# Two attention stages with their TensorE products cut into four 32-column strips

## The chip, the cores and the metric

The kernel runs on one core of a Trainium2 chip. The metric is the device time of one execution in microseconds; below stand the median of three runs and one execution taken by the hardware profiler.

## The reference

Inputs are x of 8 batches x 1024 tokens x 256 features and the weights of two attentions and of one mixture of experts. Four residual stages follow one another, each on the layer norm of what came before:

```python
x = x + attn_a(layernorm(x), ...)   # 16 heads of 16; each token looks back by 40 fixed offsets (0..32, 48, 64, ..., 384), gate, output projection
x = x + ffn(layernorm(x), ...)      # 32 experts, each takes its 8 best tokens of a batch
x = x + attn_b(layernorm(x), ...)   # 16 heads of 16, causal attention over all 1024 tokens, output projection
x = x + ffn(layernorm(x), ...)
```

Both attentions take a softmax over scores q k, the first with a bias for each offset.

## The kernel before

Each engine has a program of its own, written out step by step from one list (`band_schedule`, `dense_schedule`); semaphores order the engines against each other. Work goes by batch `b` (8) and group `g` of four heads (4), so each attention stage has 32 periods. PSUM holds three slots of 128 x 1024 fp32 and the output accumulator. Every step of TensorE that fills a slot waits until the step three before it has been taken out by VectorE or ScalarE (`slot_free`).

*Precision.* q and k are split into three bf16 parts; six pairs of parts stand on 96 partitions, so that one bf16 product gives a score in near fp32 precision. Three further partitions (99 in all) hold ones and the negated row maximum in three parts: the maximum is subtracted within the product. Projections, value products and transposes are fp32; an fp32 matmul is two records in the trace, each with a weight load and two passes over the moving columns.

*First attention* (`band_attention`). A step `mx` (maxima) puts the bias and a mask into the slot by three products with an identity (L629, L632: 128 stationary columns), then adds the scores of near tokens, 32 blocks of 32 stationary columns (`products`, L582), and those of the far offsets, 16 blocks of 64 stationary columns (L587). VectorE reduces the maxima. A step `S` does the same products transposed, without the three first. Per period: four of each, then the value products `PV` (L665, L675: fp32, 17 stationary columns a head, one head to each of the four 32-partition strips of the accumulator). `fp` (L639) sorts the far maxima, `mt` (L648) turns the maxima into rows, and DMAs (SyncE's queue) put the rows into the operands of the next group's `S`. Between the value products stand quarters of projections of the next batch or the last one (`quarter`: q and k L595, v, gate and output L603, their bias L604 by a product of 3 rows and 128 columns). GpSimd and ScalarE reorder the operands by residue (L512, L888).

*Second attention* (`dense_attention`). Units of 1024 score columns: for each group 18 units `S` (99 rows) and 18 units `mx` (96 rows) of the next group. Unit 0 has the eight diagonal tiles (L1209, 128 columns each, for `mx` after two mask products, L1205); the others have products of 128 to 512 moving columns (L1217). ScalarE takes the exponential of each `S`, VectorE the maxima of each `mx`; `PV` (L1237) is as in the first stage, 17 columns a head in four strips. Projections are L1255 (q, k), L1266 (v), L1298 (output) with biases L1268 and L1300; `mt` (L1274) is one transpose of 96 columns.

Of the kernel before, what the change touches and what calls it, by code (L numbers as in the profile page):

```python
# [18 lines left out]
P = 128  # L19
F32 = mybir.dt.float32  # L20
BF16 = mybir.dt.bfloat16
# [4 lines left out]
B, N, D = 8, 1024, 256  # L26
NT = N // P
KD = D // P
H, HD = 16, 16
G, HG = 4, 4  # L30
PARTS = 3
# [72 lines left out]
LINKS = 16  # L104
RES = N // LINKS
NEAR = [off for off in OFFSETS if off <= BLK]
FAR = [off for off in OFFSETS if off > BLK]
LINE_N, LINE_F = 96, 128


def hold(eng, sem, n):
# [118 lines left out]
def band_attention(nc, x, x_sb, stats, ident, w, scratch):  # L230
# [26 lines left out]
    with ExitStack() as ctx:  # L257
# [3 lines left out]
        wqk = sb("wqk", [P, 2, KD, H, HD])  # L261
        wv = sb("wv", [P, KD, D])
        wout = sb("wout", [P, KD, D])
# [4 lines left out]
        bias_rows = row_home[0:PARTS, 0, 0:3 * D].rearrange("a (n d) -> a n d", n=3)  # L268
        ones_rows = row_home[0:PARTS, 1, 0:P]
        neg_rows = row_home[AT_ROWS:AT_ROWS + HG * PARTS, :, :]  # L270
        ident16 = sb("ident16", [P, P], BF16)
        bias_k = sb("bias_k", [P, H, 2, 64])
        bias_q = [sb(f"bias_q{kind}", [P, H, 64], BF16) for kind in range(2)]
        before_first = sb("before_first", [P, 64], BF16)
        perm = sb("perm", [P, P + LINKS], BF16)
# [198 lines left out]
        with nc.Block() as block:  # L474
# [85 lines left out]
            def _(pe):  # L560
# [14 lines left out]
                def products(dst, rows, h, left, right, ahead, start):  # L575

                    for blk in range(N // BLK):
                        i, c = divmod(blk, 4)
                        lo = BLK * blk - (0 if ahead else BLK)
                        first, last = max(lo, 0), min(lo + 64, N)  # L580
                        at = 64 * i - lo
                        pe.matmul(dst[BLK * c:BLK * (c + 1), at + first:at + last], left[0][rows, h, BLK * blk:BLK * (blk + 1)],  # L582
                                  right[0][rows, h, first:last], start=start, stop=True, skip_group_check=True)
                    for r in range(LINKS):
                        pair, r2 = divmod(r, 2)
                        at = 512 + 64 * pair
                        ins = pe.matmul(dst[RES * r2:RES * (r2 + 1), at:at + 64], left[1][rows, h, RES * r:RES * (r + 1)],  # L587
                                        right[1][rows, h, RES * r:RES * (r + 1)], start=start, stop=True, skip_group_check=True)
                    return ins

                def quarter(dst, kind, b, part, n):

                    if kind in ("q", "k"):
                        kd, c = divmod(n, 2)
                        return pe.matmul(dst[:, c * 512:(c + 1) * 512],  # L595
                                         wqk[:, "qk".index(kind), kd, 8 * part:8 * part + 8, :].rearrange("p h d -> p (h d)"),
                                         zT[:, kd, c * 512:(c + 1) * 512], start=kd == 0, stop=kd == KD - 1)
                    weights, bias = {"v": (wv, V_BIAS), "gate": (wgate, GATE_BIAS), "op": (wout, OUT_BIAS)}[kind]
                    to = dst[:, n * D:(n + 1) * D]
                    for kd in range(KD):  # L600
                        tokens = flatT[:, (n * KD + kd) * P:(n * KD + kd + 1) * P] if kind == "op" else \
                            zT[:, kd, (4 * part + n) * P:(4 * part + n + 1) * P]
                        pe.matmul(to, tokens, weights[:, kd, :], start=kd == 0, stop=False)  # L603
                    return pe.matmul(to, ones_rows[:, :], bias_rows[:, bias, :], start=False, stop=True)  # L604

                def stacks(b, g, pair):
                    near, far = ring(b, g, pair, BY_TOKEN), ring(b, g, pair, BY_RESIDUE)
# [2 lines left out]
                for step in seq:  # L610
# [8 lines left out]
                    elif kind == "mx":  # L619
# [6 lines left out]
                        pe.wait_ge(turned_k, turns)  # L626
                        dst = slot_free(step)
                        for kind in range(2):
                            pe.matmul(dst[:, 512 * kind:512 * (kind + 1)], ident16[:, :],  # L629
                                      bias_q[kind][:, HG * g + h, :].unsqueeze(1).to_broadcast([P, NT, 64]), start=True, stop=False,  # L630
                                      skip_group_check=True)
                        pe.matmul(dst[:, 0:64], ident16[:, :], before_first[:, :], start=False, stop=False, skip_group_check=True)  # L632
                        products(dst, slice(0, QK_ROWS), h % 2, q, k, False, False).then_inc(filled, 1)
                    elif kind == "fp":
                        _, b, g = step
                        pe.wait_ge(spread_steps, 3 * count("fparts", "fparts", b, g))
                        dst = slot_free(step)
                        for pair in range(NT):
                            ins = pe.matmul(dst[:, 0:64], perm[:, LINKS - 2 - 2 * pair:LINKS - 2 - 2 * pair + P], far_parts[:, pair, :, :].rearrange("p t c -> p (t c)"),  # L639
                                            start=pair == 0, stop=pair == NT - 1)  # L640
                        ins.then_inc(filled, 1)
                    elif kind == "mt":
                        _, b, g = step
# [389 lines left out]
def dense_attention(nc, x_sb, stats, ident, w, scratch):  # L1033
# [32 lines left out]
    with ExitStack() as ctx:  # L1066
# [53 lines left out]
        with nc.Block() as block:  # L1120
# [56 lines left out]
            def _(pe):  # L1177
# [11 lines left out]
                for step in seq:  # L1189
# [3 lines left out]
                    if kind in ("S", "mx"):  # L1193
# [8 lines left out]
                        own, other, rows = (k_stack[n], q_stack[n], ALL_ROWS) if kind == "S" else (q_stack[n], k_stack[n], QK_ROWS)  # L1202
                        if u == 0:
                            for c in range(2 if kind == "mx" else 0):
                                pe.matmul(dst[:, 512 * c:512 * (c + 1)], ident16[:, :], later[:, :].unsqueeze(1).to_broadcast([P, 4, P]),  # L1205
                                          start=True, stop=False, skip_group_check=True)
                            for tile in range(NT):
                                mine = slice(P * tile, P * tile + P)
                                ins = pe.matmul(dst[:, mine], own[0:rows, h, mine], other[0:rows, h, mine], start=kind == "S", stop=True,  # L1209
                                                skip_group_check=True)  # L1210
                        for head, base in ((h, 0),) if 0 < u < 4 else ((2 * h, 0), (2 * h + 1, 512)) if u else ():
                            for tile, at in (unit_tiles if kind == "S" else unit_maxima)(u):
                                at += base
                                lo, end = (P * tile + P, N) if kind == "S" else (0, P * tile)
                                while lo < end:
                                    top = min(end, lo + 512 - at % 512)
                                    ins = pe.matmul(dst[:, at:at + top - lo], own[0:rows, head, P * tile:P * tile + P],  # L1217
                                                    other[0:rows, head, lo:top], start=True, stop=True)
                                    at, lo = at + top - lo, top
                        ins.then_inc(filled, 1)  # L1220
                    elif kind == "PV":
# [27 lines left out]
                    elif kind in ("q", "k"):  # L1249
# [2 lines left out]
                        dst = slot_free(step)  # L1252
                        for kd in range(KD):
                            for c in range(2):
                                ins = pe.matmul(dst[:, c * 512:(c + 1) * 512],  # L1255
                                                wqk[:, "qk".index(kind), kd, 8 * half:8 * half + 8, :].rearrange("p h d -> p (h d)"),
                                                zT[:, kd, c * 512:(c + 1) * 512], start=kd == 0, stop=kd == KD - 1)
                        ins.then_inc(filled, 1)
                    elif kind == "v":
                        _, b, i4 = step  # L1260
# [2 lines left out]
                        for i in range(4):  # L1263
                            tile = slice((4 * i4 + i) * P, (4 * i4 + i + 1) * P)
                            for kd in range(KD):
                                pe.matmul(dst[:, i * D:(i + 1) * D], zT[:, kd, tile], wv[:, kd, :, :].rearrange("p h d -> p (h d)"),  # L1266
                                          start=kd == 0, stop=False)
                            ins = pe.matmul(dst[:, i * D:(i + 1) * D], ones_rows[:, :], bias_rows[:, V_BIAS, :], start=False, stop=True)  # L1268
                        ins.then_inc(filled, 1)
                    elif kind == "mt":  # L1270
                        _, b, g = step
                        pe.wait_ge(mred_done, count("mred", "mred", b, g))
                        dst = slot_free(step)
                        pe.transpose(dst[:, :].bitcast(BF16)[0:PARTS * HG * NT, 0:P], neg_parts[:, :, :, :].rearrange("p a h i -> p (a h i)"),  # L1274
                                     ident16[:, :]).then_inc(filled, 1)
                    elif kind == "ot":
                        _, b, g = step
                        pe.wait_ge(ote_done, count("ote", "ote", b, g))
# [13 lines left out]
                    elif kind == "op":  # L1292
                        _, b, i4 = step
                        pe.wait_ge(taken_act, count("taken_act", "at", b, i4))
                        dst = slot_free(step)
                        for i in range(4):
                            for kd in range(KD):
                                pe.matmul(dst[:, i * D:(i + 1) * D], flatT[:, (i * KD + kd) * P:(i * KD + kd + 1) * P], wout[:, kd, :],  # L1298
                                          start=kd == 0, stop=False)
                            ins = pe.matmul(dst[:, i * D:(i + 1) * D], ones_rows[:, :], bias_rows[:, OUT_BIAS, :], start=False, stop=True)  # L1300
                        ins.then_inc(filled, 1)

            @block.vector
# [748 lines left out]
```

## Time and profile before

| | us |
|---|---|
| median of 3 runs (lowest, highest) | 3425.82 (3421.61, 3429.7) |
| span of the profiled execution | 3413.9 |
| TensorE matmul busy | 2844.6 (83%), 45724 matmuls |
| VectorE, ScalarE, GpSimd busy | 1633.9 (48%), 1439.6 (42%), 811.5 (24%) |
| first attention, main part | 120 to 1337 |
| second attention, main part | 1760 to 3115 |

In the trace's rows a time of a matmul reaches from its start to its modelled end, so that matmuls overlap; how fast they follow each other is read from the starts. A form like `99*128 99x512 bf16` is rows * stationary columns, then rows x moving columns.

### The profile page before, as it was taken

The page shows a single profiled execution, that of the slowest core. Times are in us where ns is not written, and L with a number is a line of the kernel's source. Part 1 is how long each engine was busy: PE and PEld are TensorE (multiplying, and loading weights), DVE is VectorE, ACT ScalarE, POOL GpSimd, SP SyncE. Part 2 cuts the span into 40 slices and gives each one's busy share as a digit, 9 for nine tenths or more (in the row PEclk, how much of TensorE's full clock was granted, in tenths as well). Part 3 has the DMA queues.
Part 4 walks back from the last instruction along what each step waited for, and adds up shares of the span by engine and source line. Part 5 has one row for each costly group of instructions (what it writes and reads, how often), then busy time and mean ns, then how long its engine had stood idle before and what let it go on. Part 6 is the DMA issues. An engine that isn't in the chain of part 4 may idle for free. (4 is left out here: it accounts for less than half of the span.)

```text
span 3413.9 us, 101201 instructions
## 1 busy us (share of the span) xinstructions
PE 2844.6 (83%) x45724; PEld 1618.9 (47%) x45724; DVE 1633.9 (48%) x2745; ACT 1439.6 (42%) x1425; POOL 811.5 (24%) x567
## 2 busy tenths in 40 slices
PE   2678888978888886799569899998989899997897
PEld 1455565656556565434334444444444444443444
DVE  2444343344344443600666666666666666663401
ACT  1454444444534443410235454555545554554401
POOL 3343433343434331000412122222222221210002
PEclk9789898889889897899679999999999999998998
DMA  6332323243333331388042122222222221221397
GB/s 182 87 101 66 95 66 97 70 107 77 94 79 80 82 93 36 115 326 365 19 92 58 44 57 55 57 57 57 57 57 57 56 58 40 56 39 58 152 420 268
DMA packets 233548, 344.23 MB, mean 101 GB/s; under 512 B 113691, under 2 KB 142181, under 8 KB 216741
## 3 DMA queue, kind: packets, MB, share of 16 engines
q1 hardware_dynamic: 207892, 310.02, 31.2%
q10 hardware_dynamic: 25232, 27.83, 3.4%
q8 instruction: 357, 5.85, 0.7%
q14 instruction: 67, 0.54, 0.1%
HBM read 266.15 MB, written 69.24 MB: 98 GB/s over the span
## 5 line engine op out<-in xcount | busy, mean ns | idle before, releaser
L1362 DVE TENSOR_REDUCE b_tops<-b_slot 128x8 f32<-128x1024 f32 x576 | 680.1, 1219 | 358.1 <-PE b_slot L1217 180.6
L1403 ACT ACTIVATE b_probs<-b_slot 128x1024 f32<-128x1024 f32 x576 | 583.0, 1023 | 550.7 <-PE b_slot L1217 396.3
L512 POOL COPY a_q_far<-a_q_near 96x1024 bf16<-96x1024 bf16 x128 | 259.1, 2054 | 344.4 <-PE a_slot L587 218.6
L1164 POOL TENSOR_SCALAR_AFFINE_SELECT b_probs<-b_probs 128x1024 f32<-128x1024 f32 x128 | 139.8, 1093 | 808.1 <-ACT b_probs L1403 808.1
L1237 PE MATMUL b_outT_ps<-b_probs,b_v 128*17 128x128 f32 (+3 forms) x4608 | 319.4, 385 | 6.2 <-ACT b_probs L1403 5.6
L1217 PE MATMUL b_slot<-b_q_stack,b_k_stack 99*128 99x512 bf16 (+3 forms) x1280 | 275.6, 322 | 43.5 <-DVE b_tops L1362 32.8
L888 ACT ACTIVATE a_k_far<-a_k_near 96x1024 bf16<-96x1024 bf16 x128 | 258.3, 2068 | 102.7 <-DMA a_k_near<-parts_near_dram 93.6
L1217 PE MATMUL b_slot<-b_k_stack,b_q_stack 96*128 96x512 bf16 (+3 forms) x1280 | 266.7, 323 | 29.4 <-DVE b_tops L1362 20.6
L788 DVE TENSOR_TENSOR a_probs<-a_slot,a_bias_k 128x1024 f32<-128x1024 f32 x128 | 154.4, 1217 | 182.9 <-PE a_slot L587 182.7
L797 DVE TENSOR_REDUCE a_tops<-a_slot 128x16 f32<-128x1024 f32 x128 | 156.3, 1221 | 135.9 <-PE a_slot L587 134.9
L851 ACT ACTIVATE a_probs<-a_probs 128x1024 f32<-128x1024 f32 x128 | 133.3, 1053 | 176.3 <-DVE a_probs L788 153.8
L1217 PEld LDWEIGHTS b_slot<-b_q_stack,b_k_stack 99*128 99x128 bf16 x1280 | 107.1, 100 | 204.7 <-DVE b_tops L1362 61.8
L1896 PE MATMUL f_ps<-f_w_ring,f_hidT 128*32 128x256 f32 x1024 | 184.0, 380 | 2.1 <-ACT f_hidT L1944 2.1
L1217 PEld LDWEIGHTS b_slot<-b_k_stack,b_q_stack 96*128 96x128 bf16 x1280 | 97.5, 98 | 185.4 <-DVE b_tops L1362 61.5
L665 PEld LDWEIGHTS a_outT_ps<-a_probs,a_v_near 128*17 128x17 f32 x8448 | 129.8, 103 | 84.6 <-issue 73.9
L665 PE MATMUL a_outT_ps<-a_probs,a_v_near 128*17 128x64 f32 (+1 forms) x8448 | 153.8, 228 | 16.1 <-issue 10.9
L629 PE MATMUL a_slot<-a_bias_q,a_ident 128*128 128x512 bf16 x256 | 100.3, 482 | 80.1 <-POOL a_q_far L512 50.0
L595 PE MATMUL a_slot<-a_zT,a_wqk 128*128 128x512 f32 x256 | 149.8, 691 | 5.7 <-issue 3.0
L1875 PE MATMUL f_ps<-f_w_ring,f_lhs 128*32 128x512 f32 x512 | 146.9, 606 | 7.9 <-POOL f_lhs L1854 7.9
L1976 DVE TENSOR_TENSOR f_pre<-f_ps,f_b1T 128x128 f32<-128x128 f32 x32 | 7.8, 286 | 299.9 <-PE f_ps L1884 299.9
L1237 PEld LDWEIGHTS b_outT_ps<-b_probs,b_v 128*17 128x17 f32 x4608 | 96.3, 96 | 113.8 <-issue 69.3
L675 PE MATMUL a_outT_ps<-a_probs,a_v_far 128*17 128x32 f32 x8192 | 110.5, 198 | 37.1 <-issue 36.7
(226 smaller groups left out, 4262.0 us busy)
## 6 DMA issues: line engine op xcount, KB each, us to landing
f_w_ring<-in_L_ffn_w_dram SPq DMA_DIRECT2D x128, 1024.0 KB, 9.9
parts_near_dram<-a_parts ACTq DMA_DIRECT2D x96, 256.0 KB
parts_dram<-b_parts SPq DMA_DIRECT2D x96, 256.0 KB
a_k_near<-parts_near_dram SPq DMA_DIRECT2D x128, 128.0 KB, 3.0
b_k_stack<-parts_dram SPq DMA_DIRECT2D x64, 256.0 KB, 6.8
a_q_near<-parts_near_dram SPq DMA_DIRECT2D x64, 192.0 KB, 2.9
b_q_stack<-parts_dram SPq DMA_DIRECT2D x32, 384.0 KB, 4.5
values_dram<-a_v_stage SPq DMA_DIRECT2D x16, 544.0 KB, 3.8
```

Of the source, the lines that this page charges most:

```text
L512: pool.tensor_copy(q_far[far][0:QK_ROWS, h, :].rearrange("p (r a) -> p r a", r=LINKS), q_near[near][0:QK_ROWS, h, :].rearrange("p (a r) -> ...
L595: return pe.matmul(dst[:, c * 512:(c + 1) * 512], wqk[:, "qk".index(kind), kd, 8 * part:8 * part + 8, :].rearrange("p h d -> p (h d)"), zT ...
L665: ins = pe.matmul(outT_ps[BLK * h:BLK * h + HD + 1, lo:top], v_near[:, c, blk % 4, (HD + 1) * h:(HD + 1) * (h + 1)], probs[h][:, at:at + t ...
L788: ins = dve.tensor_tensor(probs[h][:, :].rearrange("p (k t c) -> p k t c", k=2, c=64), src[:, :].rearrange("p (k t c) -> p k t c", k=2, c=64),
L797: ins = dve.tensor_reduce(tops[:, h, :, :].rearrange("p k t -> p (k t)"), src[:, :].rearrange("p (t c) -> p t c", c=64), AX.X, ALU.max)
L888: act.activation(k_far[far][0:QK_ROWS, h, :].rearrange("p (r a) -> p r a", r=LINKS), k_near[near][0:QK_ROWS, h, :].rearrange("p (a r) -> p ...
L1217: ins = pe.matmul(dst[:, at:at + top - lo], own[0:rows, head, P * tile:P * tile + P], other[0:rows, head, lo:top], start=True, stop=True)
L1237: ins = pe.matmul(outT_ps[32 * h:32 * h + HD + 1, first:last], v1[b % 2][:, j, HG * g + h, :], src[:, base + first:base + last], start=u = ...
L1362: ins = dve.tensor_reduce(out, src, AX.X, ALU.max)
L1403: act.activation(probs_of(b, g, u, h)[:, :], slot_of(step)[:, :], ACT.Exp).then_inc(taken_act, 1)
L1875: ins = pe.matmul(bank[n][32 * j:32 * j + 32, :], lhs1[half][:, kd, j, :], w1_ring[:, j, kd, n * 512:(n + 1) * 512], start=kd == 0, stop=k ...
L1896: ins = pe.matmul(bank[4 + half][32 * j:32 * j + 32, 0:D], hidT[half][:, c, j, :], w2_ring[:, j, c, :], start=c == 0, stop=c == HE // P - 1)
```

## The change

A helper issues one product as four: 32 stationary columns each, to the four strips of 32 partitions of the same PSUM tile, with the same moving operand. It replaces the products of L595, L603, L629, L632, L639, L1205, L1209, L1217, L1255, L1266 and L1298; the far products (L587) go from one of 64 columns to two of 32, and the second stage's `mt` from one transpose to three. The bias products, all other transposes, the value products and the expert stages stay.

```diff
+STRIP = 32
+def strips(pe, dst, left, right, start, stop, skip=False):
+    for c in range(0, P, STRIP):
+        ins = pe.matmul(dst[c:c + STRIP], left[:, c:c + STRIP], right, start=start, stop=stop, skip_group_check=skip)
+    return ins
...
-                        ins = pe.matmul(dst[RES * r2:RES * (r2 + 1), at:at + 64], left[1][rows, h, RES * r:RES * (r + 1)],
-                                        right[1][rows, h, RES * r:RES * (r + 1)], start=start, stop=True, skip_group_check=True)
+                        for half in range(0, RES, STRIP):
+                            to = RES * r2 + half
+                            ins = pe.matmul(dst[to:to + STRIP, at:at + 64], left[1][rows, h, RES * r + half:RES * r + half + STRIP],
+                                            right[1][rows, h, RES * r:RES * (r + 1)], start=start, stop=True, skip_group_check=True)
...
-                        pe.matmul(to, tokens, weights[:, kd, :], start=kd == 0, stop=False)
-                    return pe.matmul(to, ones_rows[:, :], bias_rows[:, bias, :], start=False, stop=True)
+                        strips(pe, to, tokens, weights[:, kd, :], kd == 0, False, True)
+                    return pe.matmul(to, ones_rows[:, :], bias_rows[:, bias, :], start=False, stop=True, skip_group_check=True)
...
-                                ins = pe.matmul(dst[:, mine], own[0:rows, h, mine], other[0:rows, h, mine], start=kind == "S", stop=True,
-                                                skip_group_check=True)
+                                ins = strips(pe, dst[:, mine], own[0:rows, h, mine], other[0:rows, h, mine], kind == "S", True, True)
...
-                                    ins = pe.matmul(dst[:, at:at + top - lo], own[0:rows, head, P * tile:P * tile + P],
-                                                    other[0:rows, head, lo:top], start=True, stop=True)
+                                    ins = strips(pe, dst[:, at:at + top - lo], own[0:rows, head, P * tile:P * tile + P],
+                                                 other[0:rows, head, lo:top], True, True, True)
...
-                        pe.transpose(dst[:, :].bitcast(BF16)[0:PARTS * HG * NT, 0:P], neg_parts[:, :, :, :].rearrange("p a h i -> p (a h i)"),
-                                     ident16[:, :]).then_inc(filled, 1)
+                        for a in range(PARTS):
+                            ins = pe.transpose(dst[:, :].bitcast(BF16)[STRIP * a:STRIP * a + HG * NT, 0:P],
+                                               neg_parts[:, a, :, :].rearrange("p h i -> p (h i)"), ident16[:, :])
+                        ins.then_inc(filled, 1)
...
```

The other products named above are replaced by `strips` in the same way.

## Rows read from the trace of the kernel before

**Rows 1.** Busy time by stretch: span of it, engines' busy us (instructions), clock, DMA share, GB/s.

```profile
120.00:1337.00 1217.00, 1009.07 (x30732) 694.95 (x30736) 523.80 (x785) 551.50 (x427) 434.74 (x273) 0.88 0.33 83
...
1760.00:3115.00 1355.00, 1232.66 (x10585) 604.56 (x10576) 844.76 (x1171) 698.22 (x701) 254.83 (x180) 0.99 0.24 52
```

**Rows 2.** Waits of TensorE, 1760 to 3115: who for whom, us in all, times, longest.

```profile
PE b_slot L1217 <- DVE b_tops L1362: 49.8, 118, 0.5
```

**Rows 3.** Waits of TensorE, 120 to 1337.

```profile
PE a_slot L582 <- DMA a_q_far<-a_row_home: 43.9, 16, 10.1
PE a_slot L629 <- POOL a_q_far L512: 35.4, 15, 5.4
PE a_outT_ps L675 <- issue: 32.0, 33, 2.3
...
PE a_outT_ps L665 <- issue: 10.9, 11, 1.9
```

**Rows 4.** Timeline of TensorE in the second attention: start, us, form, count, idle before.

```profile
2208.34 0.61 PE L1217 MATMUL b_slot<-b_q_stack,b_k_stack 99*128 99x512 bf16 x3 [0.35 <-DVE b_tops L1362]
2208.88 0.84 PE L1237 MATMUL b_outT_ps<-b_probs,b_v 128*17 128x384 f32 x8
2209.65 0.61 PE L1217 MATMUL b_slot<-b_k_stack,b_q_stack 96*128 96x512 bf16 x3
2210.09 1.03 PE L1266 MATMUL b_slot<-b_wv,b_zT 128*128 128x256 f32 x4
2211.06 0.28 PE L1268 MATMUL b_slot<-b_bias_rows,b_ones_rows 3*128 3x256 bf16 x1
2211.26 1.13 PE L1266 MATMUL b_slot<-b_wv,b_zT 128*128 128x256 f32 x4
2212.33 0.28 PE L1268 MATMUL b_slot<-b_bias_rows,b_ones_rows 3*128 3x256 bf16 x1
```

**Rows 5.** Timeline of TensorE in the first attention, two places.

```profile
841.38 0.41 PE L582 MATMUL a_slot<-a_q_near,a_k_near 99*32 99x64 bf16 x32
841.73 0.44 PE L587 MATMUL a_slot<-a_q_far,a_k_far 99*64 99x64 bf16 x16
842.10 0.61 PE L629 MATMUL a_slot<-a_bias_q,a_ident 128*128 128x512 bf16 x2
...
897.91 1.12 PE L595 MATMUL a_slot<-a_zT,a_wqk 128*128 128x512 f32 x2
898.97 1.99 PE L665 MATMUL a_outT_ps<-a_probs,a_v_near 128*17 128x64 f32 x136
```

**Rows 6.** Instruction queue q8, 120 to 1337, then 1760 to 3115: packets, MB, share.

```profile
q8 instruction: 242, 3.96, 1.4%
...
q8 instruction: 84, 1.38, 0.4%
```

**Rows 7.** Timeline of TensorE at the end of the first attention.

```profile
1326.78 0.36 PE L665 MATMUL a_outT_ps<-a_probs,a_v_near 128*17 128x64 f32 x16 [1.60 <-issue]
1327.08 0.41 PE L639 MATMUL a_slot<-a_far_parts,a_perm 128*128 128x64 bf16 x8
1327.42 1.12 PE L675 MATMUL a_outT_ps<-a_probs,a_v_far 128*17 128x32 f32 x104
1330.35 0.37 PE L675 MATMUL a_outT_ps<-a_probs,a_v_far 128*17 128x32 f32 x24 [1.82 <-issue]
...
1333.92 0.54 PE L675 MATMUL a_outT_ps<-a_probs,a_v_far 128*17 128x32 f32 x41 [1.75 <-issue]
```

**Rows 8.** Timeline of TensorE, two stalls, 128 matmuls from the first to the second.

```profile
906.45 0.59 PE L595 MATMUL a_slot<-a_zT,a_wqk 128*128 128x512 f32 x1 [1.35 <-issue]
...
910.31 0.89 PE L675 MATMUL a_outT_ps<-a_probs,a_v_far 128*17 128x32 f32 x74 [0.36 <-issue]
```

**Rows 9.** Busy time by group of one batch (g = 0 to 3), columns as in rows 1.

```profile
757.60:801.00 43.40, 40.75 (x1044) 29.05 (x1044) 17.59 (x20) 18.20 (x15) 14.00 (x9) 0.96 0.36 89
801.00:841.40 40.40, 36.10 (x1005) 23.90 (x1005) 16.80 (x26) 19.91 (x16) 14.08 (x9) 0.87 0.26 58
841.40:883.50 42.10, 31.58 (x979) 20.66 (x979) 17.74 (x27) 18.98 (x15) 18.23 (x11) 0.80 0.41 105
883.50:913.80 30.30, 22.99 (x960) 16.55 (x964) 14.52 (x18) 15.30 (x12) 11.47 (x8) 0.94 0.38 95
```

More of the change, by code:

```diff
@@ L594, in quarter @@
                         kd, c = divmod(n, 2)
-                        return pe.matmul(dst[:, c * 512:(c + 1) * 512],
-                                         wqk[:, "qk".index(kind), kd, 8 * part:8 * part + 8, :].rearrange("p h d -> p (h d)"),
-                                         zT[:, kd, c * 512:(c + 1) * 512], start=kd == 0, stop=kd == KD - 1)
+                        return strips(pe, dst[:, c * 512:(c + 1) * 512],
+                                      wqk[:, "qk".index(kind), kd, 8 * part:8 * part + 8, :].rearrange("p h d -> p (h d)"),
+                                      zT[:, kd, c * 512:(c + 1) * 512], kd == 0, kd == KD - 1, True)
                     weights, bias = {"v": (wv, V_BIAS), "gate": (wgate, GATE_BIAS), "op": (wout, OUT_BIAS)}[kind]
@@ L628, in _ @@
                         for kind in range(2):
-                            pe.matmul(dst[:, 512 * kind:512 * (kind + 1)], ident16[:, :],
-                                      bias_q[kind][:, HG * g + h, :].unsqueeze(1).to_broadcast([P, NT, 64]), start=True, stop=False,
-                                      skip_group_check=True)
-                        pe.matmul(dst[:, 0:64], ident16[:, :], before_first[:, :], start=False, stop=False, skip_group_check=True)
+                            strips(pe, dst[:, 512 * kind:512 * (kind + 1)], ident16[:, :],
+                                   bias_q[kind][:, HG * g + h, :].unsqueeze(1).to_broadcast([P, NT, 64]), True, False, True)
+                        strips(pe, dst[:, 0:64], ident16[:, :], before_first[:, :], False, False, True)
                         products(dst, slice(0, QK_ROWS), h % 2, q, k, False, False).then_inc(filled, 1)
@@ L638, in _ @@
                         for pair in range(NT):
-                            ins = pe.matmul(dst[:, 0:64], perm[:, LINKS - 2 - 2 * pair:LINKS - 2 - 2 * pair + P], far_parts[:, pair, :, :].rearrange("p t c -> p (t c)"),
-                                            start=pair == 0, stop=pair == NT - 1)
+                            ins = strips(pe, dst[:, 0:64], perm[:, LINKS - 2 - 2 * pair:LINKS - 2 - 2 * pair + P],
+                                         far_parts[:, pair, :, :].rearrange("p t c -> p (t c)"), pair == 0, pair == NT - 1, True)
                         ins.then_inc(filled, 1)
@@ L1204, in _ @@
                             for c in range(2 if kind == "mx" else 0):
-                                pe.matmul(dst[:, 512 * c:512 * (c + 1)], ident16[:, :], later[:, :].unsqueeze(1).to_broadcast([P, 4, P]),
-                                          start=True, stop=False, skip_group_check=True)
+                                strips(pe, dst[:, 512 * c:512 * (c + 1)], ident16[:, :], later[:, :].unsqueeze(1).to_broadcast([P, 4, P]),
+                                       True, False, True)
                             for tile in range(NT):
                                 mine = slice(P * tile, P * tile + P)
-                                ins = pe.matmul(dst[:, mine], own[0:rows, h, mine], other[0:rows, h, mine], start=kind == "S", stop=True,
-                                                skip_group_check=True)
+                                ins = strips(pe, dst[:, mine], own[0:rows, h, mine], other[0:rows, h, mine], kind == "S", True, True)
                         for head, base in ((h, 0),) if 0 < u < 4 else ((2 * h, 0), (2 * h + 1, 512)) if u else ():
@@ L1254, in _ @@
                             for c in range(2):
-                                ins = pe.matmul(dst[:, c * 512:(c + 1) * 512],
-                                                wqk[:, "qk".index(kind), kd, 8 * half:8 * half + 8, :].rearrange("p h d -> p (h d)"),
-                                                zT[:, kd, c * 512:(c + 1) * 512], start=kd == 0, stop=kd == KD - 1)
+                                ins = strips(pe, dst[:, c * 512:(c + 1) * 512],
+                                             wqk[:, "qk".index(kind), kd, 8 * half:8 * half + 8, :].rearrange("p h d -> p (h d)"),
+                                             zT[:, kd, c * 512:(c + 1) * 512], kd == 0, kd == KD - 1, True)
                         ins.then_inc(filled, 1)
@@ L1265, in _ @@
                             for kd in range(KD):
-                                pe.matmul(dst[:, i * D:(i + 1) * D], zT[:, kd, tile], wv[:, kd, :, :].rearrange("p h d -> p (h d)"),
-                                          start=kd == 0, stop=False)
-                            ins = pe.matmul(dst[:, i * D:(i + 1) * D], ones_rows[:, :], bias_rows[:, V_BIAS, :], start=False, stop=True)
+                                strips(pe, dst[:, i * D:(i + 1) * D], zT[:, kd, tile], wv[:, kd, :, :].rearrange("p h d -> p (h d)"),
+                                       kd == 0, False, True)
+                            ins = pe.matmul(dst[:, i * D:(i + 1) * D], ones_rows[:, :], bias_rows[:, V_BIAS, :], start=False, stop=True,
+                                            skip_group_check=True)
                         ins.then_inc(filled, 1)
@@ L1297, in _ @@
                             for kd in range(KD):
-                                pe.matmul(dst[:, i * D:(i + 1) * D], flatT[:, (i * KD + kd) * P:(i * KD + kd + 1) * P], wout[:, kd, :],
-                                          start=kd == 0, stop=False)
-                            ins = pe.matmul(dst[:, i * D:(i + 1) * D], ones_rows[:, :], bias_rows[:, OUT_BIAS, :], start=False, stop=True)
+                                strips(pe, dst[:, i * D:(i + 1) * D], flatT[:, (i * KD + kd) * P:(i * KD + kd + 1) * P], wout[:, kd, :],
+                                       kd == 0, False, True)
+                            ins = pe.matmul(dst[:, i * D:(i + 1) * D], ones_rows[:, :], bias_rows[:, OUT_BIAS, :], start=False, stop=True,
+                                            skip_group_check=True)
                         ins.then_inc(filled, 1)
```

## The prediction

> **What bounds the kernel now.** I read the busy time by stage first, then who TensorE waits for in the two attention stages, then the timeline of a few microseconds of each, and last the DMA queues. The two attention stages take 1217 and 1355 of the 3414 us, and TensorE is busy 83% and 91% of them; no other engine passes 62% [rows 1]. In the second stage what TensorE does wait for is small pieces: 118 waits on one reduction of VectorE, 50 us in all, 0.5 us the longest [rows 2]. So there TensorE sets the pace, and time taken from it is mostly time won. The first stage differs: beside waits for the transposed maxima (DMA, 44 us) there are waits put down to "issue", where the engine had nothing to wait for and still did not go on: 32 and 11 us at the two lines of the value products alone [rows 3].
>
> The reader should now find in the timeline what a change of array shape costs. A step of 1024 score columns takes 0.44 us to the next start when a full-width product follows (2209.65 to 2210.09), which is its streaming, 1024 columns at 2.4 GHz = 0.43; it takes 0.54 when a 17-column product follows (2208.34 to 2208.88). Back again, eight records of 384 fp32 columns need 0.64 in two rounds (384 x 2 / 2.4 GHz each) and take 0.77 [rows 4]. So a change of shape costs 0.10 us. The eight records also show that four strips run side by side: one after another they would need 2.56 us.
>
> **What goes.** Along the timeline I count the places where neighbouring matmuls differ in shape (at most 32, 64 or 128 stationary columns; 3 rows or about 100): 1403 in the first stage, 987 in the second. With the change 513 and 406 are left: transposes stay at 128 columns, and the bias product keeps 3 rows and 128 columns, with a change on either side. Removed are 890 and 581, at 0.098 us: 87 and 57 us.
>
> The first fp32 weight load after a shape change isn't hidden: four records start to finish 0.97 us behind a full-width step and 1.07 behind the bias product [rows 4]; a woven quarter of a projection takes 1.06 for 0.85 of streaming, 0.10 of it the change of shape back [rows 5]. A 32-column load behind a change costs at most the 0.03 left over in the 0.77 above. I count 238 and 90 such loads: at 0.075 us 18 and 7 us (ends: 0 and 0.10 each).
>
> Streaming stays: four strips pass the same moving columns side by side, as the value products do in fp32 and the near products in bf16 (32 matmuls of 64 columns in 0.35 us to the next start, against 0.85 one after another; the 16 of 64 stationary columns in 0.37) [rows 5]. Three transposes for one in the second stage's row step, 32 times, I put at nothing: they go to three strips. So TensorE is relieved of 105 us in the first stage and of 64 in the second.
>
> **What is added: instructions.** Every strip is a weight load and a matmul of its own. One instruction queue moves in step with TensorE, whatever the others do: 242 packets of 16.4 KB for the 30732 matmuls of the first stage, one for 127 matmuls, 84 for the 10585 of the second [rows 6, 1]. What a packet costs when it is late is seen at the end of the first stage: three stalls put down to "issue", at 1326.78, 1330.35 and 1333.92, and between the first two exactly 16 + 8 + 104 = 128 matmuls: 3.57 us a packet, of which the engine worked about half [rows 7]. A second pair, at 906.45 and 910.31, again 128 matmuls apart, gives 3.86 [rows 8]. I take the mean, 3.72; these are the ends of the price.
>
> Matmuls added in one group of four heads in the first stage: 8 steps x 16 far products, 4 maxima steps x 9, 24 in the far maxima: 188; and 24 for each q or k, 48 for each v, gate or output half. The four groups of a batch have 8, 4, 3 and 1 units of 24 of these: 192, 96, 72, 24. From 1044, 1005, 979 and 960 [rows 9] that makes 1424, 1289, 1239 and 1172 matmuls, or 11.1, 10.1, 9.7 and 9.2 packets. At 3.72 us: 41.4, 37.5, 36.0 and 34.1 us, against periods of 43.4, 40.4, 42.1 and 30.3 now [rows 9]. The fourth is the tell-tale: it has the least other work, and its 7.5 packets x 3.72 = 27.9 us already fill 92% of its 30.3. If a stream bound by its packets keeps that 8.6% of pauses (waits in which nothing is drawn), the four become 45.0, 40.7, 39.1 and 37.0: 161.8 us for the batch's 156.2. The 13.1 us that a batch is relieved of (111 shape changes, 30 loads) don't come off again: where packets set the pace, they are already spent inside these numbers, and the third group without packets, 42.1 less its share of 3.8, would end at 38.3, under its 39.1. First stage: +5.6 x 8 = +45 us.
>
> What the Trainium skill says of this (Runtime: NRT & Kernel Launch, section Instruction fetch mechanics): the sequencer fetches the next block of 256 instructions by its own DMA while the current one runs, and crossing into it is mostly hidden. The block's size agrees with 127 matmuls a packet; the stalls of 1.6 to 1.8 us do not agree with hidden. By the rule this term would be 0, the first stage would win, and the sum is that of the first rival.
>
> Second stage: each group has 40 + 32 matmuls of scores, the same of maxima and 8 of mask, all four-fold, and its projections; some 530 more in 42 us, so 84 packets become about 216 in 1355 us, 6.3 us apiece, far from 3.9. The relief counts here. Not in full: VectorE is busy 62% of the stage, and TensorE stands behind its reductions in 118 of its 1152 steps already (18 of each kind in 32 groups) [rows 1, 2]; each step that comes sooner meets them more often. I take two thirds of 64, -43 us (ends: a third and all, -21 and -64). The expert stages don't change.
>
> Sum against the profiled span of 3413.9: +45 - 43 = +2, so 3416; the median of the runs lies 11.9 us above that span, hence **3428 us**.
>
> **Rivals.** *Packets stay hidden.* The extra packets land where TensorE waits for something else. Then the first stage gives two thirds of its 105, -70, and the whole is 3426 - 70 - 43 = 3313. Even with packets at the low price and no pause, three of four groups come out under their present length. For: 44 us of DMA waits and 35 of GpSimd's in rows like these can cover packets [rows 3]. Against: the fourth group, 92% full.
>
> *Packets cost more.* At 3.86 us with the same pauses a batch takes 167.9 us, +11.7 x 8 = +94; if VectorE also keeps two thirds of the second stage's relief, 3426 + 94 - 21 = 3499. It decides as soon as a packet costs over 3.72 us, the price at which both stages cancel. For: the stage runs at a DMA share of 0.33 [rows 1], the cheap pair stood in a quiet stretch.
>
> *Strips load one after another.* If the four 32-column loads of a 128-column product don't overlap, 128 moving columns (0.053 us at 2.4 GHz) cost the 0.10 of an exposed load: for the 2560 such products of the second stage +0.047 each = +120 us, 3548. Against: 32 loads and matmuls in 0.35 us [rows 5]. The Trainium skill (TensorEngine Tiling (Array Packing), Feature Incompatibilities) does say that column tiling excludes the fast weight load; no row here shows a cost of it.
>
> *The shape change is paid anyway*, since numbers of rows (96, 99, 128) or types also count as a shape: the rows deny it (fp32 behind bf16 at full width took 0.44) [rows 4].
>
> **How the numbers follow.** Cancelling within 40 us either way: 0.46 (own range 3388 to 3468). Hidden packets: 0.22. Dear packets: 0.26. Loads in turn: 0.04. No shape change removed: 0.02, no change. What a measurement of this kernel can tell from no change is about 0.2%, 7 us. Of the first case 0.18 falls below that, 0.10 inside, 0.18 above. Faster 0.40, same 0.12, slower 0.48. The range from 3350 to 3490 leaves the far part of the two big rivals out.
>
> **What would show it.** In the profile after: second stage, score step to value product 0.43 instead of 0.54, the stage some 40 us shorter, VectorE's share up. First stage: over 300 packets, "issue" waits of TensorE well above now, 128 matmuls between stalls, the fourth group 36 to 38 us, the third 38 to 40. Wrong if the "issue" waits don't grow, if strips show 0.2 us or more for four of 512 columns one after another, or if the second stage doesn't shorten because VectorE's reductions end last.

## The result, and the profile after

The changed kernel takes 3584.03 us (median of 4 runs, 3574.83 to 3605.45) against 3423.72: ratio 1.0479, 95% interval 1.044 to 1.0519. Forecast were 3428 us, 3350 to 3490. The profiled execution's span is 3576.6 us, 162.7 more than before.

The page, TensorE's busy time and the instruction queue:

```profile
PE 2779.1 (78%) x71772; PEld 1617.0 (45%) x71772; DVE 1637.9 (46%) x2745; ACT 1436.1 (40%) x1425; POOL 813.2 (23%) x567
...
q8 instruction: 560, 9.18, 1.1%
```

TensorE is busy 65 us less than before, and the kernel is 163 us longer: time was lost while the array stood still. By stretch, the two attentions, then one batch's four groups of the first, the same batch as in [rows 9]:

```profile
120.00:1415.00 1295.00, 954.80 (x39261) 655.69 (x39262) 527.08 (x785) 551.90 (x426) 435.71 (x273) 0.86 0.31 79
1845.00:3285.00 1440.00, 1223.81 (x26788) 653.71 (x26781) 846.01 (x1172) 694.92 (x702) 255.95 (x181) 0.95 0.23 50
...
789.93:840.31 50.38, 40.77 (x1425) 25.40 (x1426) 17.60 (x20) 18.30 (x15) 13.81 (x9) 0.90 0.32 81
840.31:882.37 42.06, 32.40 (x1286) 21.47 (x1289) 16.62 (x26) 19.94 (x16) 14.13 (x9) 0.92 0.22 53
882.37:923.96 41.59, 27.51 (x1240) 19.50 (x1232) 17.85 (x27) 18.12 (x14) 18.32 (x11) 0.88 0.41 107
923.96:959.13 35.17, 23.07 (x1168) 17.19 (x1168) 14.24 (x18) 16.32 (x13) 11.47 (x8) 0.85 0.33 83
```

Against [rows 1] the first attention is 78 us longer and the second 85; what lies outside the two takes 842 us in both. In the first TensorE's busy time fell by 54 us and its idle time (length less busy) rose from 208 to 340; in the second it went from 122 to 216. The waits name it, of the first attention (120 to 1415), then of the second (1845 to 3285):

```profile
PE a_slot L597 <- issue: 72.1, 36, 3.7
PE a_outT_ps L684 <- issue: 65.4, 47, 2.7
PE a_slot L590 <- issue: 51.0, 32, 4.2
PE a_outT_ps L674 <- issue: 29.0, 36, 1.9
...
PE a_slot L115 <- issue: 20.8, 21, 2.5
...
PE b_slot L115 <- issue: 70.8, 25, 5.2
PE b_slot L115 <- DVE b_tops L1374: 53.5, 130, 0.6
...
PE b_outT_ps L1245 <- issue: 14.7, 5, 4.3
```

(L590 and L597 are the near and far products, L674 and L684 the value products, L115 is the helper; L1245 is L1237 of before.) "Issue" had 32 and 11 us at the value products of the first attention [rows 3], 60 in all its rows there, and no row in the second. Now it has 238 us in the five rows of the first (249 in all) and 86 in the second, where VectorE's row hardly moved [rows 2]. The packets of q8 in the same two stretches, against 242 and 84 [rows 6]:

```profile
q8 instruction: 308, 5.05, 1.7%
...
q8 instruction: 210, 3.44, 1.0%
```

What the strips do to the array is as forecast. A score step is followed by a value product after 0.44 us, where it was 0.54 [rows 4], and the four strips of 512 columns pass side by side:

```profile
2270.49 0.61 PE L115 MATMUL b_slot<-b_q_stack,b_k_stack 99*32 99x512 bf16 x12
2270.93 1.04 PE L1245 MATMUL b_outT_ps<-b_probs,b_v 128*17 128x128 f32 x32
```

The end of the first attention, as in [rows 7]: the stalls follow each other at 3.74, 3.62, 3.60 and 3.47 us, a packet's 127 or 128 matmuls apart, so the price of a late packet held too:

```profile
1396.60 1.88 PE L674 MATMUL a_outT_ps<-a_probs,a_v_near 128*17 128x64 f32 x128 [0.24 <-issue]
1400.34 1.36 PE L674 MATMUL a_outT_ps<-a_probs,a_v_near 128*17 128x64 f32 x87 [1.87 <-issue]
...
1403.96 1.25 PE L684 MATMUL a_outT_ps<-a_probs,a_v_far 128*17 128x32 f32 x120 [1.88 <-issue]
...
1407.56 0.46 PE L657 MATMUL a_slot<-a_ident,a_neg_parts 128*12 128x128 bf16 x6 [1.93 <-issue]
...
1411.03 0.26 PE L684 MATMUL a_outT_ps<-a_probs,a_v_far 128*17 128x32 f32 x9 [1.80 <-issue]
```

**One long stall of the second attention.** At the beginning of each group the eight steps of unit 0 follow each other: 32 strips of 128 columns for each `S`, 8 + 32 for each `mx`. Timelines of TensorE and of SyncE's DMA issues, then the DMA queues from 2249.6 to 2254.7 and from 2254.7 to 2257.0, then busy time in three stretches (the last three columns are granted clock, DMA share and GB/s):

```profile
2247.72 0.63 PE L115 MATMUL b_slot<-b_q_stack,b_k_stack 99*32 99x128 bf16 x32 [0.43 <-DMA b_q_stack<-b_neg_rows]
...
2252.13 0.61 PE L115 MATMUL b_slot<-b_q_stack,b_k_stack 99*32 99x128 bf16 x30
2257.91 0.29 PE L115 MATMUL b_slot<-b_q_stack,b_k_stack 99*32 99x128 bf16 x2 [5.16 <-issue]
2257.91 1.14 PE L115 MATMUL b_slot<-b_later,b_ident 128*32 128x512 bf16 x8
2258.74 2.02 PE L115 MATMUL b_slot<-b_k_stack,b_q_stack 96*32 96x128 bf16 x44
2260.45 1.16 PE L115 MATMUL b_slot<-b_q_stack,b_k_stack 99*32 99x128 bf16 x32
2261.30 1.16 PE L115 MATMUL b_slot<-b_k_stack,b_q_stack 96*32 96x512 bf16 x12
```

```profile
2244.61 0.76 SPq L1161 DMA_DIRECT2D b_q_stack<-b_neg_rows  x1
2245.88 1.27 SPq L1156 DMA_DIRECT2D b_q_stack<-parts_dram  x3
2247.19 1.84 SPq L1156 DMA_DIRECT2D b_k_stack<-parts_dram  x4
```

```profile
q1 hardware_dynamic: 552, 0.98, 107.0%
...
q8 instruction: 1, 0.02, 4.5%
```

```profile
2249.60:2254.70 5.10, 3.14 (x146) 2.10 (x136) 3.26 (x3) 1.94 (x2) 2.08 (x2) 1.00 1.07 193
2254.70:2257.90 3.20, 0.00 (x0) 0.00 (x0) 0.00 (x0) 0.00 (x0) 0.00 (x0) 0.76 0.27 37
2257.90:2263.20 5.30, 5.29 (x114) 3.72 (x117) 3.06 (x3) 2.05 (x2) 1.56 (x2) 0.50 0.01 3
```

Read it in this order. The burst begins as the rows of maxima arrive, at 2247.72, and from 1.8 us ahead of it until 1.3 us into it SyncE issues seven stack loads of the group after next. TensorE passes a packet boundary at some 2249.6 (128 matmuls ahead of the stall). For the next 5.1 us the sixteen DMA engines move loads at 193 GB/s and queue q8 moves nothing; its packet starts only as they run out, at 2254.75 by the trace's records, and 3.2 us later TensorE goes on. The clock, 1.00 ahead of the stall, is 0.50 behind it (1.2 for 2.4 GHz): the 44 strips at 2258.74 take 2.02 us from first start to last end, and the same 44 take 1.24 in e5 below, without a stall. In the changed kernel 22 stalls of the second attention are over 2 us, 77 us of the 86. In each the packet started 2.8 to 6.7 us behind the last boundary, with 140 to 210 GB/s of transfers between. They fall at the group's first steps (18) or some 10 us later (4): in every second group SyncE issues stores of the next batch's q and k (L1144) right behind the rows of maxima, and the stack loads 9 to 10 us behind them instead of 1.3; three of the 18 fall behind such stores.

### The profile page after: what moved, and what is told of

Same layout as the page of the kernel before. It is cut to its first block and busy times, and to the rows that moved or that the text cites. A ratio compares the mean times of both kernels' runs of the same rounds, so it can differ in the third digit from the quotient of the medians.

```text
span 3576.6 us, 153297 instructions
## 1 busy us (share of the span) xinstructions
PE 2779.1 (78%) x71772; PEld 1617.0 (45%) x71772; DVE 1637.9 (46%) x2745; ACT 1436.1 (40%) x1425; POOL 813.2 (23%) x567
## 5 line engine op out<-in xcount | busy, mean ns | idle before, releaser
L115 PE MATMUL b_slot<-b_q_stack,b_k_stack 99*32 99x128 bf16 (+3 forms) x9216 | 378.5, 284 | 73.2 <-issue 27.2
L115 PE MATMUL b_slot<-b_k_stack,b_q_stack 96*32 96x128 bf16 (+3 forms) x9216 | 375.3, 287 | 65.1 <-issue 37.8
L1245 PE MATMUL b_outT_ps<-b_probs,b_v 128*17 128x128 f32 (+3 forms) x4608 | 323.0, 386 | 25.1 <-issue 14.7
L115 PEld LDWEIGHTS b_slot<-b_k_stack,b_q_stack 96*32 96x32 bf16 x9216 | 208.0, 101 | 223.5 <-issue 91.5
L115 PEld LDWEIGHTS b_slot<-b_q_stack,b_k_stack 99*32 99x32 bf16 x9216 | 194.3, 100 | 248.4 <-issue 82.9
L674 PE MATMUL a_outT_ps<-a_probs,a_v_near 128*17 128x64 f32 (+1 forms) x8448 | 172.9, 234 | 31.8 <-issue 29.0
L674 PEld LDWEIGHTS a_outT_ps<-a_probs,a_v_near 128*17 128x17 f32 x8448 | 153.7, 107 | 86.3 <-issue 79.2
L684 PE MATMUL a_outT_ps<-a_probs,a_v_far 128*17 128x32 f32 x8192 | 116.7, 200 | 70.5 <-issue 70.1
L1245 PEld LDWEIGHTS b_outT_ps<-b_probs,b_v 128*17 128x17 f32 x4608 | 120.5, 99 | 84.4 <-ACT b_probs L1415 36.7
L115 PE MATMUL a_slot<-a_bias_q,a_ident 128*32 128x512 bf16 x1024 | 109.2, 506 | 60.7 <-POOL a_q_far L520 43.4
L115 PE MATMUL a_slot<-a_zT,a_wqk 128*32 128x512 f32 x1024 | 146.0, 641 | 3.8 <-issue 2.4
```

The source lines that it names most:

```text
L115: ins = pe.matmul(dst[c:c + STRIP], left[:, c:c + STRIP], right, start=start, stop=stop, skip_group_check=skip)
L674: ins = pe.matmul(outT_ps[BLK * h:BLK * h + HD + 1, lo:top], v_near[:, c, blk % 4, (HD + 1) * h:(HD + 1) * (h + 1)], probs[h][:, at:at + t ...
L1245: ins = pe.matmul(outT_ps[32 * h:32 * h + HD + 1, first:last], v1[b % 2][:, j, HG * g + h, :], src[:, base + first:base + last], start=u = ...
```

## The experiments

All are ratios to the kernel before in runs on the same chip (3423 to 3427 us there), with 95% intervals.

| run | us | ratio |
|---|---|---|
| e1 first attention changed alone | 3492.02 | 1.0223 (1.0184 to 1.0263) |
| e2 second attention changed alone | 3505.19 | 1.0253 (1.0203 to 1.0302) |
| e3 = e2, stack loads later in the order | 3506.03 | 1.0243 (1.0201 to 1.0285) |
| e4 = e2, unit 0 at 128 columns | 3404.86 | 0.9943 (0.9922 to 0.9965) |
| e5 = e2, stack loads held | 3403.45 | 0.9931 (0.9909 to 0.9953) |
| e6 kernel before, stack loads held | 3430.16 | 1.0019 (1.0 to 1.0037) |
| e7 = e1, far products at 64 columns | 3446.58 | 1.0059 (1.0037 to 1.008) |
| e8 = e4, stack loads held | 3385.84 | 0.9883 (0.9856 to 0.9909) |
| e9 whole change, stack loads held | 3479.28 | 1.0167 (1.0139 to 1.0195) |
| e10 only projection quarters of the first | 3416.80 | 0.9979 (0.9961 to 0.9997) |
| e11 = e8 + e10 | 3375.38 | 0.9864 (0.984 to 0.9889) |
| e12 = e1, V loaded once | 3493.06 | 1.0208 (1.0184 to 1.0233) |
| e13 kernel before, V loaded once | 3420.02 | 0.9979 (0.9965 to 0.9992) |

**e1 and e2: each attention alone.** The edit: the diff in one of the two functions only.

> The change in the first attention alone. Both theories: the loss of 78 us that the two profiles show up to the end of the first attention stays and the second stage is that of before, so about 3503 us (3490 to 3515). If the two stages' losses are not independent (the first leaving a queue or a clock behind for the second), it lies elsewhere.

> The change in the second attention alone: 3424 + 84 = about 3508 us (3495 to 3520), with some 86 us of TensorE waits put down to issue in that stage and a granted clock of 0.93 to 0.95 there.

Both lose: 2.2% and 2.5%, together 4.8%, which is the whole. So the stages' losses add up, and the forecast's gain of 43 us in the second does not exist in it even by itself.

**e3: stack loads seven beats later in the written order.**

```diff
-            if ahead[0] < B:
-                seq.append(("stack",) + ahead)
...
+                if n == 6 and ahead[0] < B:
+                    seq.append(("stack",) + ahead)
```

> The change in the second attention alone, and the loads of a group's operand stacks (1.3 MB for the group after the next) issued at the seventh of its 18 beats instead of ahead of the first, where the instructions come densest. Theory of late instruction packets, held up by these loads on the same DMA engines: the issue waits of the stage fall to less than half, the half-clock stretches behind them too, 3440 to 3470 us. Rival, the strips themselves cost TensorE time (moving operand read four times, weight loads that do not overlap): as the second attention alone, 3500 to 3515 us.

Nothing moved, which looks like the end of the theory. But the experiment was empty. SyncE's queue isn't paced by the beats, only by its semaphores, and the loads were issued where they had been, behind the rows of maxima (at this burst of the changed kernel 1.27 us, here the same; in the other groups within 0.2 us of e2):

```profile
2178.93 0.76 SPq L1161 DMA_DIRECT2D b_q_stack<-b_neg_rows  x1
2180.20 1.27 SPq L1156 DMA_DIRECT2D b_q_stack<-parts_dram  x3
```

**e4: unit 0 and its mask back to 128 columns.** The edit: the `strips` of `u == 0` become the products of before; 6912 of the 16960 added matmuls go.

> The change in the second attention alone, but with unit 0 (mask products and the eight diagonal tiles of each head) left at 128 columns: of 16900 added matmuls 6900 stay away, those of the densest beats, and most shape changes beside the value products are still gone. Late packets: next to no issue waits, the relief of some 40 us shows, 3385 to 3400 us. Strips that cost TensorE time: 10000 added matmuls remain, no gain, 3440 us or more.

From 82 us slower to 18 faster, 5 us above the range expected, while the strips of all other units stay. The loss comes with the strips of unit 0, whose score products are the shortest; 14 us of stalls are left (10.1 at the helper, 4.3 at the value products).

**e5 and e6: the loads really kept out of the burst**, in e2 and, as a control, in the kernel before. The edit is the order of e3 and this wait:

```diff
+                        if now := before(b, g, 2):
+                            sp.wait_ge(filled, count("filled", "S", *now, 1, 2))
```

> Second attention changed alone, and the loads of the stacks two groups ahead really kept out of the burst: SyncE waits, ahead of each stack load, for the products of the group's seventh beat. In the kernel with the late place in the order these loads had still started at the group's first beat (2180.2 us, 1.3 us behind the rows of maxima), since nothing paced SyncE; that run moved nothing and told nothing. Theory A, the loads hold the instruction packet back (in the stalls of over 2 us the packet started 2.4 to 5.8 us behind the last boundary, with 178 to 212 GB/s of loads between): the long stalls at the group's first beats go, 3425 to 3455 us. Theory B, a packet has its price whatever the loads do: 3500 to 3510 us, as without the hold.

> The kernel before with the same hold on the stack loads and nothing else, as a control. Theory A and B alike: 84 packets in the second attention were all there in time, so the hold is worth nothing, 3415 to 3430 us. If the hold itself costs (stacks late for the next group's maxima), it is above 3430.

One wait on SyncE, with no instruction taken from TensorE, brings e2 from 3505 to 3403 us, further than I expected; in the kernel before the same wait is worth nothing (3430.16, at the upper end of what was expected). The same burst in e5, with the loads issued 20 us behind the rows of maxima, then the waits for the helper (1760 to 3115) and the second attention as a whole:

```profile
2143.60 0.63 PE L115 MATMUL b_slot<-b_q_stack,b_k_stack 99*32 99x128 bf16 x32 [0.43 <-DMA b_q_stack<-b_neg_rows]
...
2148.01 0.62 PE L115 MATMUL b_slot<-b_q_stack,b_k_stack 99*32 99x128 bf16 x32
2148.45 0.61 PE L115 MATMUL b_slot<-b_later,b_ident 128*32 128x512 bf16 x8
2148.89 1.24 PE L115 MATMUL b_slot<-b_k_stack,b_q_stack 96*32 96x128 bf16 x44
```

```profile
2140.50 0.76 SPq L1163 DMA_DIRECT2D b_q_stack<-b_neg_rows  x1
2160.53 1.26 SPq L1158 DMA_DIRECT2D b_q_stack<-parts_dram  x3
```

```profile
PE b_slot L115 <- issue: 16.2, 15, 2.3
```

```profile
1680.40:3127.00 1446.60, 1259.44 (x27871) 661.70 (x27871) 895.35 (x1224) 714.40 (x721) 276.50 (x192) 0.97 0.26 55
```

In e2 the waits on issue are 74.9 + 11.1 us and the same stretch, first slot to last, is this:

```profile
1678.50:3218.80 1540.30, 1288.94 (x27871) 682.55 (x27871) 895.95 (x1224) 713.57 (x721) 276.44 (x192) 0.94 0.24 52
```

So 94 us shorter: about 70 of stalls, and the clock can account for the rest. Summed over the trace's clock records, this stretch has 171 us at half clock in e2 and 95 in e5 (89 in the kernel before, 198 in the changed one). At half clock a step of 32 strips took 0.85 us to the next start (2260.45 to 2261.30 above), at full clock 0.44, so the 76 us are worth some 38 at most. Three stalls of 2.1 to 2.3 us are left in e5, in groups where the stores of q and k run during the burst; the wait doesn't hold those.

**e7: far products of the first attention at 64 columns**, `products` as before the change.

> First attention changed alone, but with the products of the far keys left at 64 columns: 4096 fewer matmuls than the 9100 or so added, 32 packets fewer, and up to 512 shape changes come back. Theory, packets set the pace of the first attention at some 3.7 us each: 32 packets are worth 60 to 118 us and the shapes cost 26 to 51 us, so 3400 to 3460 us against 3492. Rival, the strips themselves cost array time and the packets are mostly hidden: 3515 to 3545 us.

49 of e1's 69 us go (each against its own runs of before) with 4096 matmuls, 32 packets, although up to 512 changes of shape come back: 1.5 us net a packet. TensorE's waits on issue in this stage (120 to 1415) go from 244 us in e1 to 148. The rival is out, and the array doesn't lose by the far strips either: in the changed kernel 32 of them take 0.33 us to the next start, where the 16 of 64 columns took 0.37 ahead of the same product [rows 5].

```profile
795.21 0.51 PE L597 MATMUL a_slot<-a_q_far,a_k_far 99*32 99x64 bf16 x32
795.54 0.61 PE L115 MATMUL a_slot<-a_bias_q,a_ident 128*32 128x512 bf16 x8
```

**e8 and e9: the hold beside other versions.** e8 is e4 with the hold, e9 the whole change with it.

> Second attention with unit 0 and its mask left at 128 columns, plus the hold on the stack loads. Theory A: the 14 us of stalls left there shrink a little, 3390 to 3405 us. Theory B: no change from 3405 us, 3398 to 3412.

> The whole change with the stack loads of the second attention held to the seventh beat. Theory, the hold is worth in it what it was worth in the second attention alone (3505 to 3403 us, 102 us) and the first attention keeps its own price (69 us alone): 3584 less 102 is 3482, range 3470 to 3498 us, second attention near 1450 us long, first near 1390. Rival, the two stages share one loss: above 3510.

e8 is another 19 us under e4 and under the range of either theory: e4's last 14 us of stalls in this stage are gone (no such row among the 40 largest waits). Its second attention is 1422.50 us against the 1466.2 of before from first slot to last: 44 us shorter, about what was forecast for this stage, though unit 0 keeps its shapes here; it also has 27 us less at half clock (62 for 89), worth up to half of that. e9 comes out 3 us from the sum of the parts.

```profile
1678.90:3101.40 1422.50, 1250.49 (x20959) 642.64 (x20959) 895.04 (x1224) 716.60 (x721) 276.44 (x192) 0.98 0.25 56
```

**e10 and e11: a version that beats both.** The edit of e10: `quarter` alone takes `strips`, 3072 matmuls more; e11 puts it on e8.

> The kernel before with only the woven projection quarters of the first attention in strips: 3072 matmuls more, 24 packets, and two shape changes fewer at each of up to 448 quarters. Theory, packets at 3.7 us where the pieces fall in starved stretches, hidden where a quarter's long matmuls cover them: 27 to 89 us lost, 45 to 90 us gained, so 3385 to 3440 us, likeliest 3415. Rival, strips give the array nothing: 3450 or more.

> The fastest so far (second attention with unit 0 at 128 columns and the hold, 3386 us) plus the projection quarters of the first attention in strips. 3386 plus whatever the quarters alone change against the kernel before: 3345 to 3400 us, likeliest 3375.

e10 gains a little (0.2%, the interval ends at 0.9997). e11 is the fastest kernel of the study: 1.4% under the kernel before, 5.8% under the changed one.

**e12 and e13: the first attention without most loads of V.** SyncE loads V for the first group only and every later group multiplies by that V, so the output is another.

```diff
+                        if (b, g) != (0, 0):
+                            continue
...
-                            pe.wait_ge(v_in, VIN * count("vin", "vin", b, g))
+                            pe.wait_ge(v_in, VIN)
```

> First attention changed alone, with the loads of V into the near and far layouts made for the first group only; later groups reuse the first group's V, so the values are not those of the reference, and some 16 MB of loads are gone. In the trace of the first attention changed alone 39 of 179 starved packets started over 1.5 us behind the boundary, with 179 GB/s of loads between, 39 us late in all. Theory, the missing part of the first attention's price is packets started late behind loads: 10 to 35 us less than 3492, so 3455 to 3482 us, where the kernel before without these loads does not move. Rival, the loads have no part in the first attention's price: 3488 to 3497.

> Control: the kernel before with the same loads of V left out (values not those of the reference). What this moves is worth of the loads themselves, not of packets: 3405 to 3425 us expected by both, since the kernel before has few starved packets.

A miss: 17 MB of loads fewer, and the first attention's loss stays (2.1% against 2.2%), while the control moves by 7 us. These loads have no part in it that the runs show: in the trace of e12 no fewer packets start late (51 over 1.5 us behind their boundary, for 38 in e1).

## Why the prediction was wrong

**The step that failed** is the one on the second stage: "84 packets become about 216 in 1355 us, 6.3 us apiece, far from 3.9. The relief counts here." The counts were right (210 packets in the stretch shown); the mean was the wrong thing to compare. Where unit 0 runs a packet is used up not in 6.3 us but in 2.9 (2249.6 to the standstill at 2252.5), and it isn't there within 3.7 but within 8.3 (2257.9), because its transfer starts behind a megabyte of loads. The burst and the loads at a group's start are both in the trace of before, and the forecast looked at neither:

```profile
2226.17 1.26 SPq L1147 DMA_DIRECT2D b_q_stack<-parts_dram  x3
2227.48 1.84 SPq L1147 DMA_DIRECT2D b_k_stack<-parts_dram  x4
...
2228.26 0.62 PE L1209 MATMUL b_slot<-b_q_stack,b_k_stack 99*128 99x128 bf16 x8 [0.54 <-DMA b_q_stack<-b_neg_rows]
```

Instead of -43 the stage gave +85: some 86 us of stalls, about 110 us more at half clock, which cost up to half of that, and the relief against them. e4 removes the burst, e5 the loads; either alone turns the sign. A relief of the forecast's size is there once the stalls are gone (e8, -44), though part of it may be the clock, so how much the changes of shape alone are worth stays open.

The Trainium skill (Runtime: NRT & Kernel Launch, Instruction fetch mechanics) says that the next block's fetch is mostly hidden. In this stage that holds as long as the loads are away (e5: 16 us of stalls with the same instructions) and fails by 86 us when they are not (e2).

**First stage, +45 forecast, +78 measured.** The direction, the mechanism and the matmuls a group were right: 1424, 1289, 1239 and 1172 forecast, 1425, 1286, 1240 and 1168 in the windows. The lengths were 45.0, 40.7, 39.1 and 37.0 forecast, 50.4, 42.1, 41.6 and 35.2 measured: the term mis-sized is the pause of 8.6% on top of 3.72 us, 4.04 us a packet; measured are 169.2 us for 5119 matmuls, 40.0 packets, 4.23 (this batch grew by 13.0 us, the mean of the eight is 9.8). The fourth group, from which the 8.6% came, came out best (35.17 / 9.1 = 3.9), the first, with the most projection work, worst (50.38 / 11.1 = 4.5). The same error again, in small: packets don't set the pace of a whole group. Counted from the trace's records, 256 instructions to a packet, for the 308 packets of the stage: ahead of the first instruction of 160 the queue stood for over 0.6 us, 285 us in all; the other 148 are used up in 4.0 us (median) and need no price. Stretches bound by packets and stretches bound by the array add up, where I let one stand for the group. Within the 160, 118 started in time, 1.1 us behind the boundary, and are 3.6 us apart (median); 42 started over 1.5 us behind it, 48 us later in all than those in time, with 182 GB/s of transfers before them on average; such is the 4.17 us ahead of L590 at 802.22. The clock, no term of the forecast, is a second candidate: the stage has 357 us at half clock for 302 before, and the 55 more are worth up to half of that. What share of the 33 us each has was not isolated: e12 shows only that the loads of V don't cause the late starts. The loads of the near stacks, issued in 30 of those 42 stretches, were not tried.

**The rivals.** "Packets stay hidden" gave 3313 and is out as a whole. "Packets cost more" (3499) had the right sign and too little of it: the price is 3.6 to 3.7 when the transfer starts in time. What decided the second stage is not a higher price everywhere but 22 long stalls, 18 of them at a group's first steps. "Strips load one after another" is out: 32 strips of 128 columns in 0.44 us. "No shape change removed" is out: 0.44 for 0.54.

**The sum** set a loss against a gain of the same size. The loss came out at 78 for 45, the gain as a loss of 85, and the clock, which has more time at half speed where the stalls are (171 us in e2, 95 in e5), was no term of it at all.

## What to carry to other kernels

Before an edit multiplies TensorE's instructions, go to the place where matmuls are shortest and compare how long 128 of them take with how long a packet takes there, with the loads that run at that moment; a mean over a stage says nothing. If a burst of instructions and a bulk load start on the same event, give the load a wait of its own: here one such wait was worth some 100 us. And see in the trace that an edit of an order really moved the transfer before you believe a null result.

## What the hardware showed unexpectedly

The instruction packet of TensorE came late behind data, though it has a queue of its own: with 140 to 210 GB/s of transfers on the way it started 2.8 to 6.7 us behind its boundary, and it then took 2.3 to 3.2 us more until TensorE went on. In a standstill of 5.2 us the granted clock fell from 1.00 to 0.50, and the following burst ran for 5.3 us at that level. In the first attention, behind a stall in a quiet stretch, the next packet started 1.15 us (median of 45) after TensorE went on, and between the first instructions of two packets that follow each other 283 times of 307 exactly one transfer of a packet starts.
